# Rows and gated products as fp16 halves, transposed by the DMA engines, in the mixture-of-experts phases of a two-layer block

## The reference

```python
x = hidden_states.reshape(-1, h)                 # layer-normalised rows, (2048, 512)
logits = x @ router_w.T                          # 8 experts
topk_w, topk_idx = jax.lax.top_k(softmax(logits), 2)
topk_w = topk_w / jnp.sum(topk_w, axis=-1, keepdims=True)
for each expert:                                 # 512 -> 352 -> 512
    moe_out += ce[:, None] * (silu(x @ gw) * (x @ uw) @ dw)
shared = silu(x @ s_gate_w + s_gate_b) * (x @ s_up_w + s_up_b) @ s_down_w + s_down_b   # 512 -> 704 -> 512
out = moe_out + shared
```

## Time and profile before

| | |
|---|---|
| median of the runs | 1928.39 us |
| the profiled execution, and its span | 1931.55 us, 1929.5 us |
| PE busy | 1637.1 us (85%) |
| DVE, ACT, POOL busy | 1144.6, 736.0, 420.2 us |
| DMA queues' share of the 16 engines | q1 27.4%, q0 3.4% |
| granted clock of PE, mean | 0.92 |
| x_in, stage piece, gather, expert store: issue to landing | 6.3, 7, 3.7, 2.0 us |

### The profile page before, as it was taken

The page is one execution under the profiler, slowest core; times in us unless marked ns, Lnnn a source line. Parts: engine busy times, 40 slices in busy tenths (PEclk is TensorE's granted clock), DMA queues, the critical chain, the costliest instruction groups (busy, mean ns, idle before and its releaser), DMA issues. The chain is left out here.

```text
span 1929.5 us, 28443 instructions
## 1 busy us (share of the span) xinstructions
PE 1637.1 (85%) x9848; PEld 971.4 (50%) x9849; DVE 1144.6 (59%) x2251; ACT 736.0 (38%) x1363; POOL 420.2 (22%) x310
## 2 busy tenths in 40 slices
PE   2989956999829999958898875974999999999997
PEld 1778842444316666624444443632555555555554
DVE  4978843333273343356776855466677676776654
ACT  2321103323232222224332322365556566565552
POOL 1323301233451111023313211053120101201000
PEclk6989977999959999978999996787999999999999
DMA  8212224333142222253213003244235042251432
GB/s 183 65 65 88 87 100 151 108 121 107 61 129 77 88 82 82 66 190 110 67 48 104 1 22 132 77 136 105 52 70 120 16 103 59 61 120 22 88 67 55
DMA packets 207503, 168.09 MB, mean 87 GB/s; under 512 B 141538, under 2 KB 157922, under 8 KB 207282
## 3 DMA queue, kind: packets, MB, share of 16 engines
q1 hardware_dynamic: 200256, 147.02, 27.4%
q0 software_dynamic: 5680, 18.62, 3.4%
q10 hardware_dynamic: 1474, 1.21, 0.3%
HBM read 101.98 MB, written 31.28 MB: 69 GB/s over the span
## 5 line engine op out<-in xcount | busy, mean ns | idle before, releaser
L1846 POOL TENSOR_TENSOR s_h_lo<-s_h,s_h_hi 128x512 f16<-128x512 f32 x32 | 37.0, 1155 | 520.0 <-DVE s_h_hi L2080 520.0
L2098 PE MATMUL s_ring<-w_w_hi,s_xt_hi 128*128 128x512 f16 x256 | 99.3, 388 | 12.8 <-issue 12.8
L274 POOL TENSOR_TENSOR prod_lo<-prod,prod_hi 128x2304 f16<-128x2304 f32 x16 | 73.2, 4577 | 168.7 <-ACT prod_hi L307 168.7
L463 PE MATMUL ring<-prod_hi,toep 128*128 128x288 f16 x320 | 92.7, 290 | 19.5 <-DVE terms L383 11.4
L2098 PE MATMUL s_ring<-w_mu_hi,s_xt_hi 128*128 128x512 f16 x256 | 99.5, 389 | 8.1 <-DVE s_xt_lo L2001 8.1
L2099 PE MATMUL s_ring<-w_mu_lo,s_xt_hi 128*128 128x512 f16 x256 | 99.5, 389 | 0.0
L2099 PE MATMUL s_ring<-w_w_lo,s_xt_hi 128*128 128x512 f16 x256 | 99.4, 388 | 0.0
L2100 PE MATMUL s_ring<-w_mu_hi,s_xt_lo 128*128 128x512 f16 x256 | 99.3, 388 | 0.0
L2006 DVE TENSOR_REDUCE s_top<-s_lg 128x1 f32<-128x512 f32 x64 | 43.9, 686 | 93.2 <-ACT s_lg L1905 93.2
L2100 PE MATMUL s_ring<-w_w_hi,s_xt_lo 128*128 128x512 f16 x256 | 99.0, 387 | 0.0
L2098 PE MATMUL s_acc<-w_w_hi,s_g_hi 128*128 128x512 f16 x256 | 97.1, 379 | 0.2
(11 more groups left out here) (387 smaller groups left out, 4811.9 us busy)
## 6 DMA issues: line engine op xcount, KB each, us to landing
expert_rows<-e_y SPq DMA_DIRECT2D x39, 256.0 KB, 2.0
s_et<-in_L_ffn_W SPq DMA_DIRECT2D x16, 512.0 KB, 3.7
toep<-ssm_split SPq DMA_DIRECT2D x14, 512.0 KB, 5.0
stage<-in_L_ffn_gate_w SPq DMA_DIRECT2D x8, 704.0 KB, 7.1
stage<-in_L_ffn_up_w SPq DMA_DIRECT2D x8, 704.0 KB, 7.3
c_rows<-in_ctx SPq DMA_DIRECT2D x8, 512.0 KB, 10.5
x_rows<-in_x SPq DMA_DIRECT2D x8, 512.0 KB, 14.0
res<-in_x SPq DMA_DIRECT2D x128, 32.0 KB
```

The source lines that it names most:

```text
L274: nc.gpsimd.tensor_tensor(prod_lo[:, u].rearrange("p k e r -> p (k e r)"), prod[:, u, :], prod_hi[:, u].rearrange("p k e r -> p (k e r)"), ...
L463: nc.tensor.matmul(out, w_hi, hi, start=(n == 0), stop=False)
L2098: mm(out_, a[0], b_[0], start=first, stop=False)
```

## The change

1. Rows (shared phase). ACT copies `xn` to `xq_rows[:, t, 0]` (`split_rows`), DVE subtracts to `xq_rows[:, t, 1]` (`rest_of_rows`), both now from SBUF, and SP turns each row tile with one DMA transpose of 256 KB into `xt`, which has two buffers by chunk; the fp16 halves themselves (2 KB a row, as the fp32 rows had) are what is stored as `normed_rows`. PE's 16 transposes and the PSUM reads go.
2. Its place. Statistics, root, normalisation and both splits of chunk c+1 stand after m = 3 (`NORM_AT`) instead of after m = 5, on DVE and on ACT. On SP the transposes and the store stand behind the chunk's four weight pieces; for chunk 0 between the second and the third piece of the shared weights.
3. Experts. The gather brings fp16 halves, SP turns them (256 KB a tile), ACT and DVE split h in SBUF and SP turns both halves of it (192 KB). PE's four and three transposes a tile go, with the halves' PSUM reads; SP's loop is unrolled to X(n), H(n-2), S(n-3): transpose of rows, transpose of h, store.

```diff
-        xt_hi, xt_lo = sb("xt_hi", [P, KD, CH], F16), sb("xt_lo", [P, KD, CH], F16)
+        xq = sb("xq_rows", [P, 4, 2, D], F16)
+        xt = sb("xt", [P, 2, 2, KD, CH], F16)
...
+            def turn(c):
+                for t in range(4):
+                    sp.wait_ge(xq_hi_done, c * 4 + t + 1)
+                    sp.wait_ge(xq_lo_done, c * 4 + t + 1)
+                    if c >= 2 and t == 0:
+                        sp.wait_ge(routed, c - 1)
+                        sp.wait_ge(gu_done, (c - 1) * SK)
+                    sp.dma_start_transpose(xt[:, c % 2].rearrange("p q k i -> p (q k) i")[:, :, t * P:(t + 1) * P],
+                                           xq[:, t].rearrange("p q d -> p (q d)")).then_inc(turned[t], 16)
+                sp.dma_start(xn_d[:, bass.ds(c * 4, 4), :], xq[:, :, :, :].rearrange("p t q d -> p t (q d)")).then_inc(xn_stored, 16)
...
+                if n == 2:
+                    turn(0)
...
-                sp.wait_ge(normed, (c + 1) * 4)
-                sp.dma_start(xn_d[:, bass.ds(c * 4, 4), :], xn[:, :, :]).then_inc(xn_stored, 16)
                 for q in range(4):
                     sp.wait_ge(ew_lo, c * 4 + (q + 1))
                     src = (gate, up)[q % 2][bass.ds(c * 2 + q // 2, 1), :, :].rearrange("o (k p) i -> p (o k) i", p=P)
                     sp.dma_start(stage[:, q % 2, :].rearrange("p (k i) -> p k i", k=KD), src).then_inc(stage_loaded[q % 2], 16)
+                if not last:
+                    turn(c + 1)
                 sp.wait_ge(out_done, (c + 2) * 4)
...
-            def split_turned(c):
-                for b in range(KD):
-                    act.wait_ge(turned, c * KD + (b + 1))
-                    nc.scalar.activation(xt_hi[:, b, :], tr[:, b, :], ACT.Copy).then_inc(xt_hi_done, 1)
-            split_turned(0)
+            def split_rows(c):
+                for t in range(4):
+                    act.wait_ge(normed, c * 4 + t + 1)
+                    if c:
+                        act.wait_ge(turned[t], c * 16)
+                        act.wait_ge(xn_stored, (c + 1) * 16)
+                    nc.scalar.activation(xq[:, t, 0, :], xn[:, t, :], ACT.Copy).then_inc(xq_hi_done, 1)
+            split_rows(0)
...
                     act.wait_ge(h_done, c * SK + (m + 3))
                     nc.scalar.activation(h_hi[0:r, m, :], h[0:r, u, :], ACT.Copy).then_inc(h_hi_done, 1)
-                if not last:
-                    ln.root(nc, act, c + 1)
+                    if m == NORM_AT and not last:
+                        ln.root(nc, act, c + 1)
+                        split_rows(c + 1)
...
-            def rest_of_turned(c):
-                for b in range(KD):
-                    dve.wait_ge(xt_hi_done, c * KD + (b + 1))
-                    nc.vector.tensor_tensor(xt_lo[:, b, :], tr[:, b, :], xt_hi[:, b, :], ALU.subtract).then_inc(xt_lo_done, 1)
-            rest_of_turned(0)
+            def rest_of_rows(c):
+                for t in range(4):
+                    dve.wait_ge(xq_hi_done, c * 4 + t + 1)
+                    nc.vector.tensor_tensor(xq[:, t, 1, :], xn[:, t, :], xq[:, t, 0, :], ALU.subtract).then_inc(xq_lo_done, 1)
+            rest_of_rows(0)
...
-                if not last:
-                    normalise(c + 1, 1 - u)
+                    if m == NORM_AT and not last:
+                        normalise(c + 1, 1 - u)
+                        rest_of_rows(c + 1)
...
-                for b in range(KD):
-                    for t in range(4):
-                        if b == 0:
-                            pe.wait_ge(normed, c * 4 + (t + 1))
-                        if t == 0:
-                            if not (isinstance(c, int) and c == 0):
-                                pe.wait_ge(bias_added, (c - 1) * 4 + (b + 1))
-                        last = nc.tensor.transpose(tr[:, b, t * P:(t + 1) * P], xn[:, t, b * P:(b + 1) * P], k.ident[:, :])
-                    last.then_inc(turned, 1)
+                xt_hi, xt_lo = xt[:, u, 0], xt[:, u, 1]
+                for t in range(4):
+                    pe.wait_ge(turned[t], (c + 1) * 16)
+                    if c:
+                        pe.wait_ge(bias_added, (c - 1) * 4 + t + 1)
...
-        rows = sb("e_rows", [P, U, D])
-        xt_hi, xt_lo = sb("e_xt_hi", [P, U, D], F16), sb("e_xt_lo", [P, U, D], F16)
-        silu, h = sb("e_silu", [P, U, I_MOE]), sb("e_h", [P, U, I_MOE])
-        h_hi, h_lo = sb("e_h_hi", [P, U, MK, P], F16), sb("e_h_lo", [P, U, MK, P], F16)
+        rows = sb("e_rows", [P, U, 2 * D], F16)
+        xt = sb("e_xt", [P, U, 2 * KD, P], F16)
+        silu, h = sb("e_silu", [P, U, I_MOE]), sb("e_h", [P, U, MK * P])
+        hq, ht = sb("e_hq", [P, U, 2, MK * P], F16), sb("e_ht", [P, U, 2 * MK, P], F16)
         y = sb("e_y", [P, U, D])
-        turn, h_turn = ps("e_turn", [P, D]), ps("e_h_turn", [P, MK, P])
...
-                    pool.wait_ge(turned, n - U + 1)
+                    pool.wait_ge(turned[n % U], n // U * 16)
...
-                    for c in range(KD):
-                        last = nc.tensor.transpose(turn[:, c * P:(c + 1) * P], rows[:, u, c * P:(c + 1) * P], k.ident[:, :])
-                    last.then_inc(turned, 1)
...
+                    pe.wait_ge(turned[u], before * 16 + 16)
...
-                    for q in range(MK):
-                        i_ = slice(q * P, min((q + 1) * P, I_MOE))
-                        last = nc.tensor.transpose(h_turn[0:i_.stop - i_.start, q, :], h[:, u, i_], k.ident[:, :])
-                    last.then_inc(h_turned, 1)
...
+                    pe.wait_ge(h_turned[u], rounds * 16)
...
-                    act.wait_ge(turned, n + 1)
...
-                    nc.scalar.activation(xt_hi[:, r % U, :], turn[:, :], ACT.Copy).then_inc(xt_hi_done, 1)
...
-                    act.wait_ge(h_turned, n - 1)
+                    u = (r - 2) % U
+                    act.wait_ge(h_done, n - 1)
                     if early >= 5:
-                        act.wait_ge(contracted, n - 4)
-                    for rows_, blocks in parts:
-                        nc.scalar.activation(h_hi[rows_, (r - 2) % U, blocks, :], h_turn[rows_, blocks, :], ACT.Copy).then_inc(h_hi_done, 1)
+                        act.wait_ge(h_turned[u], (rounds - (1 if r % U < 2 else 0)) * 16)
+                    nc.scalar.activation(hq[:, u, 0, :], h[:, u, :], ACT.Copy).then_inc(h_hi_done, 1)
...
-                    dve.wait_ge(h_hi_done, (n - 1) * 2)
-                    for rows_, blocks in parts:
-                        nc.vector.tensor_tensor(h_lo[rows_, (r - 2) % U, blocks, :], h_turn[rows_, blocks, :],
-                                                h_hi[rows_, (r - 2) % U, blocks, :], ALU.subtract).then_inc(h_lo_done, 1)
+                    u = (r - 2) % U
+                    dve.wait_ge(h_hi_done, n - 1)
+                    nc.vector.tensor_tensor(hq[:, u, 1, :], h[:, u, :], hq[:, u, 0, :], ALU.subtract).then_inc(h_lo_done, 1)
...
-            with sp.Fori(0, TILES // U) as i:
-                for u in range(U):
-                    sp.wait_ge(y_done, i * U + (u + 1))
-                    sp.dma_start(y_out[bass.ds((i * U + u) * P, P), :], y[:, u, :]).then_inc(stored[u], 16)
+            def store(n):
+                sp.wait_ge(y_done, n + 1)
+                sp.dma_start(y_out[n * P:(n + 1) * P, :], y[:, n % U, :]).then_inc(stored[n % U], 16)
+            def turn_h(n):
+                sp.wait_ge(h_hi_done, n + 1)
+                sp.wait_ge(h_lo_done, n + 1)
+                if n >= U:
+                    sp.wait_ge(contracted, n - U + 1)
+                sp.dma_start_transpose(ht[:, n % U], hq[:, n % U].rearrange("p q i -> p (q i)")).then_inc(h_turned[n % U], 16)
+            for n in range(TILES):
+                u = n % U
+                sp.wait_ge(gathered[u], (n // U + 1) * 16)
+                if n >= U:
+                    sp.wait_ge(expanded, n - U + 1)
+                sp.dma_start_transpose(xt[:, u], rows[:, u, :]).then_inc(turned[u], 16)
+                if n >= 2:
+                    turn_h(n - 2)
+                if n >= 3:
+                    store(n - 3)
+            turn_h(TILES - 2)
+            store(TILES - 3)
+            turn_h(TILES - 1)
+            store(TILES - 2)
+            store(TILES - 1)
...
-    x1, xn, x1s, x3 = (scratch(name, (T, D)) for name in ("after_conv", "normed_rows", "after_shared", "after_xattn"))
+    x1, x1s, x3 = (scratch(name, (T, D)) for name in ("after_conv", "after_shared", "after_xattn"))
+    xn = scratch("normed_rows", (T, 2 * D), F16)
...
```

More of the change, by code:

```diff
@@ L531, in shared_phase @@
         ew_hi, ew_lo = sem("ew_hi"), sem("ew_lo")
-        normed, xn_stored, turned = sem("xn_normed"), sem("xn_stored"), sem("turned")
-        xt_hi_done, xt_lo_done = sem("xt_hi_done"), sem("xt_lo_done")
+        normed, xn_stored = sem("xn_normed"), sem("xn_stored")
+        xq_hi_done, xq_lo_done = sem("xq_hi_done"), sem("xq_lo_done")
+        turned = [sem(f"turned{t}") for t in range(4)]
```

(45 more changed lines are left out.)

13 lines of the change are left out of this document (2 added, 11 removed).

## The result

| | us | runs | ratio to before, 95% |
|---|---|---|---|
| before (first comparison) | 1930.02 | 4 | |
| the change | 1943.36 | 4 | 1.007 (1.0051 to 1.0089) |
| the change, again | 1941.85 | 7 | 1.005 (1.0027 to 1.0072) |

The forecast was 1932, a change of +3.8; measured are +13.3 and, against 1928.93, +12.9. That is slower by more than 0.5%, inside the range of 1911 to 1949 and on rival C's side. The profiled execution took 1938.46 us (span 1936.7), the lowest of its four.

What follows compares the result with a forecast made beforehand. PE was taken to bound the expert phase alone, and the shared phase with inputs coming over POOL. Expert phase -16.5 and shared phase +20.3 gave +3.8 on the median 1928.4, so 1932 us; range 1911 to 1949.

Steps and rivals of the forecast that it cites:

- rival C: Expert phase: landing of h exceeds the slack, PE waits 0.6 us a tile instead of 0.2; 1947 us, chance 0.23.
- Shared phase, the new place: Shared phase: earlier normalisation delays h(4), h(5) and the down product behind it; +20.3 us for the phase.
- Which operation is held: Shared phase: L94, the variance's first small addition with two SBUF inputs, is held by POOL until w_lo(3) ends.
- rival B: Shared phase: L94 slips between POOL operations, chain starts 4.2 us sooner, clock may hold; total 1913 us, chance 0.22.
- The store out of the first piece's way: Shared phase, chunks 1 and 2: the store no longer precedes the first weight piece, w_lo(3) comes 3.1 us sooner.
- Chunk 3, -1.4: Shared phase, chunk 3: nothing is inserted, and PE's transposes and splits at its start go; -1.4 us.
- Expert phase, PE's own time: Expert phase: without transposes a tile takes 3.60 plus 1.95, so 5.55 us instead of 6.30; 210.6 us in all.
- Does the rest come back in time: Expert phase: transposed h has 0.5 us of slack, rows 0.9; meeting the gather costs 0.2 us a tile, 7.2 us.
- Ends: Expert phase, its ends: first rows +1.5, first contract product's wait +1.4, work behind the last expand product +2.3 us.
- the term for h: Expert phase: h lands at +5.0, wanted at +5.55; the gather meeting it costs 0.2 us a tile, 7.2 us.
- the rows' term: Expert phase: the rows' transpose lands at about +6.6 and is wanted at +7.5, 0.9 us of slack, no wait counted.
- The sign of the forecast: Whole kernel: slower, by +3.8 us.

Runs made afterwards that it cites:

- e4: The changed kernel with POOL's subtraction of the fourth weight piece, w_lo(3), moved behind h_lo(5), normalisation still at m = 3; 1935.52 us.
- e8: The changed kernel with the halves of h split one step sooner, the rows' transpose also going out a step sooner; 1921.00 us, ratio 0.9957.
- e0: The changed kernel run once more without any edit; 1941.85 us.
- e10: The changed kernel with the rows' transpose one step sooner, ahead of h's transpose, the halves of h as late as before; 1929.91 us, ratio 1.0006.

## Why the prediction was right or wrong

- *Shared phase, the new place: right by mechanism; the total is near in part by luck.* Forecast were +20.3; the listing is 17.4 and 20.1 later in the two traces, the end of the shared phase 17.4 and 19.0. The variance ended with w_lo(3) in all three chunks of the first trace. Chunk end minus w_lo(3) was 429.55 - 403.94 = 25.6 in chunk 1, against 25.4. Its two parts were both off: from w_lo(3) to the end of h_lo(5) it was 413.90 - 403.94 = 9.96 us against 10.7, and fifteen matmuls went at half speed, not ten. PE's wait of "about 7" was 6.66 in chunk 1, 5.83 in chunk 2 and 4.81 in chunk 0.
- *Which operation is held: partly.* Not L94, which has 0.31 us and slips in, but one or two of the next ones: L98 and L101, L99 and L104, L96 and L98. L98 and L101 read one SBUF tensor, not two. What w_lo(3) costs is about 4.7 us over three chunks (listing at 571.42 in e4, 576.12 in the change), so rival B, which put 18.9 on it, was priced too high: e4 leaves a hold of 1.03 by h_lo(3) in chunk 1, and the slow clock that B let vanish stays. The Trainium skill (SBUF — State Buffer, SBUF: two separate sides) names DVE's two-port modes beside two SBUF inputs, and the trace agrees as far as L101, with one fp32 SBUF tensor, took 2.82 us; in which mode it ran, no trace shows.
- *The store out of the first piece's way:* 35.3 us from chunk end to w_lo(3) in chunk 1 instead of 37.7: 2.4, not 3.1; in chunk 2 33.7 instead of 37.9, 4.2. In chunk 0, where I allowed none, it was 2.4 as well. The chunks cost 5.2, 7.9 and 5.7 us, not 7.7, 7.0 and 7.0.
- *Chunk 3, -1.4:* -1.35 (17.4 behind at its end, 18.75 at its start).
- *Expert phase, PE's own time: right.* 3.60 and 1.95 hold; 5.53 is the period of e8.
- *Does the rest come back in time: this step failed.* "It lands at about +6.6 and is wanted at +7.5: 0.9 us" took the landing of 3.1 from rows 4, a phase whose engines are busy with transposes but have no gather beside them. I let the gather meet h alone, and it meets the rows of nearly every tile: they need 4.2 us in the median and land at +7.8, 0.3 too late. Of 224.2 us from the first expand product's start to the last's, 206.6 is work (38 x 3.585 + 36 x 1.955), 0.9 the fill, 2.8 the first tile's slow clock; 13.9, 0.39 a tile, are waits (16 in e0), where the sum had 7.2. Taken from start to start, some 5.9 of them stand ahead of expand products (5.8 in e0), where the sum had nothing, and some 7.9 ahead of contract products (10.4 in e0), where it had the 7.2. So the term for h came out, and by the meeting that was named; the rows' term was missing. The two hang together, since each gather goes out 0.26 us behind a landing of rows: e10 moves only the rows, and 2.0 of the 7.9 are left.
- *A term left out.* PE idles 13.36 us ahead of the first expand product and then works at a granted clock of 0.55: 6.43 us to the second instead of 3.6.
- *Ends:* the first rows +0.9 (1.5 forecast), fill 0.9 (1.4), tail 9.48 instead of 7.65, +1.8 (2.3); in e0 the tail is +3.3.

Together the expert phase gave 8.4 us in the first trace and 4.8 in e0, not 16.5. These 8.1 and 11.7 us that are lacking make the miss. The shared phase was 2.9 and 0.2 cheaper than forecast, and from the attention's first matmul to the end the two traces are 1.8 and 4.7 us shorter than that of before (1092.6 and 1089.6 against 1094.4), for which no run gives a reason. Rival C had the total (1947) but not the mechanism: h did not cost 0.6 us a tile but 0.22, the rest was the rows. The sign of the forecast stood, its size did not: +3.8 against +13.

## What to carry to other kernels

A transfer put in a loop needs its lead counted in whole steps, from the engine's queue: what is issued ahead of it there (here a store that waits for a result) sets its issue, and what is in flight beside it (here a gather) its landing. Take the landing of a transfer from a place with the same neighbours, and ask of each transfer in the loop, not of one, what it will meet. An operation moved to where its data is ready early still delays all that its engine does next; put it where the engine next waits for something else anyway.

## What the hardware showed unexpectedly

Single-tensor operations of DVE are held by POOL's subtraction as well (L101 2.82 and L98 1.04 us at 0.16 usual), while the statistics (2.46 us beside w_lo(2)) and h with one operand in PSUM (0.75) are not. The same DMA transpose of 256 KB landed after 2.8 us with no gather beside it, even 0.66 us behind a 256 KB store, after 3.1 in the median among its like, and after 3.6 to 5.5 with a gather in flight. After a wait of 3.99 and one of 1.18 us PE's steps doubled to 0.43 at a granted clock of 0.50, as after one of 6.66.
